# Layer 0 cross attention: key tiles taken in pairs, with another division of the PSUM banks

## What is computed

```python
def _L0_xattn_ref(x, latents, mask, g1, b1, g2, b2, Wq, Wkv, Wout):   # x: the context, latents: the normalised x
    heads, dim_head = (16, 64)
    xn, ln_lat = layer_norm(x, g1, b1), layer_norm(latents, g2, b2)
    q = ln_lat @ Wq
    kv = jnp.concatenate([xn, ln_lat], axis=1) @ Wkv
    k, v = jnp.split(kv, 2, axis=-1)
    q, k, v = (to_heads(q), to_heads(k), to_heads(v))
    scale = 1.0 / np.sqrt(np.sqrt(dim_head)).astype(np.float32)
    weight = jnp.einsum('bhld,bhnd->bhln', q * scale, k * scale)
    weight = jnp.where(full_mask[:, None, None, :], weight, neg)      # only context keys can be masked
    weight = jax.nn.softmax(weight.astype(jnp.float32), axis=-1)
    out = jnp.einsum('bhln,bhnd->bhld', weight, v)
    return out.transpose(0, 2, 1, 3).reshape(b, l, heads * dim_head) @ Wout
```

## Time and profile before

| what | value |
|---|---|
| median of 3 runs | 3242.64 us (3238.62 to 3245.68) |
| the profiled execution | 3243.5 us, its span 3241.8 us |
| mean granted TensorE clock | 0.943 |
| TensorE busy | 2901.1 us, 89% |
| VectorE busy | 1949.8 us, 60% |
| ScalarE busy | 1456.5 us, 45% |
| GpSimd busy | 1210.1 us, 37% |

### The profile page before, as it was taken

How to read it: one execution, slowest core, us unless ns; L and a number is a source line. 1 busy time by engine, 2 the same in 40 slices (tenths; PEclk the granted TensorE clock), 3 DMA queues, 4 the chain that set the end, 5 groups by cost and what they waited for, 6 DMA issues and landing times. The chain is left out here.

```text
span 3241.8 us, 48893 instructions
## 1 busy us (share of the span) xinstructions
PE 2901.1 (89%) x18490; PEld 1956.2 (60%) x18490; DVE 1949.8 (60%) x3101; ACT 1456.5 (45%) x2394; POOL 1210.1 (37%) x1001
## 2 busy tenths in 40 slices
PE   7869999999999979999998695999687888899977
PEld 6745555555555548888884564999465565344355
DVE  6556676676676754224218774555447858666576
ACT  3334444444444434324324373777333635355664
POOL 0026666666666640000004341566133403122232
PEclk9979999999999989999998896999798999799989
DMA  1100000000000002111101005666300000000010
GB/s 59 49 7 1 1 1 1 1 1 1 1 1 1 1 19 62 46 33 59 46 14 33 22 2 181 205 202 195 71 1 16 5 10 1 2 1 1 1 33 27
DMA packets 117131, 114.51 MB, mean 35 GB/s; under 512 B 22827, under 2 KB 102726, under 8 KB 116902
## 3 DMA queue, kind: packets, MB, share of 16 engines
q1 hardware_dynamic: 103173, 97.66, 9.7%
q0 software_dynamic: 7488, 9.48, 1.6%
q10 hardware_dynamic: 6240, 4.26, 0.4%
HBM read 100.81 MB, written 11.47 MB: 35 GB/s over the span
## 5 line engine op out<-in xcount | busy, mean ns | idle before, releaser
L827 POOL TENSOR_TENSOR acc<-acc,pf 128x512 f32<-128x512 f32 (+1 forms) x448 | 570.8, 1297 | 206.7 <-ACT pf L952 206.7
L1009 DVE TENSOR_REDUCE mxa<-ps 128x1 f32<-128x512 f32 x512 | 329.3, 684 | 290.3 <-PE ps L873 290.0
L952 ACT ACTIVATE pf<-ps 128x512 f32<-128x512 f32 x512 | 277.9, 595 | 278.0 <-PE ps L848 253.7
L861 PE MATMUL ps<-pf,v 128*64 128x512 f32 (+1 forms) x1152 | 311.7, 620 | 0.0
L3737 ACT ACTIVATE pT<-ps 128x1024 f32<-128x1024 f32 (+1 forms) x192 | 154.1, 811 | 134.3 <-PE ps L3654 133.8
L1204 POOL TENSOR_TENSOR x<-x,ys 128x256 f32<-128x256 f32 x16 | 11.8, 739 | 510.5 <-DVE ys L1409 510.5
L3750 DVE TENSOR_REDUCE mx<-ps 128x2 f32<-128x1024 f32 (+1 forms) x192 | 175.1, 951 | 45.4 <-PE ps L3641 37.4
L1858 POOL TENSOR_TENSOR e<-e,sm 128x1232 f32<-128x1232 f32 x48 | 107.9, 2247 | 168.3 <-DVE sm L2128 168.3
L2588 DVE TENSOR_TENSOR w_lo<-w2a,w_hi 128x2048 fp32r<-128x2048 f32 x39 | 89.4, 2292 | 101.5 <-ACT w_hi L2475 101.5
L2387 PE MATMUL ps<-xT,w1r 128*128 128x128 f32 x1248 | 148.2, 278 | 0.0
L2387 PEld LDWEIGHTS ps<-xT,w1r 128*128 128x128 f32 x1248 | 144.9, 195 | 0.0
(11 more groups left out here) (550 smaller groups left out, 7380.5 us busy)
## 6 DMA issues: line engine op xcount, KB each, us to landing
w1r<-in_f_w SPq DMA_DIRECT2D x39, 1024.0 KB, 5.1
w_raw<-in_c_h SPq DMA_DIRECT2D x32, 512.0 KB, 4.3
w2a<-in_f_w SPq DMA_DIRECT2D x8, 1024.0 KB, 13.0
w_raw<-in_c_w SPq DMA_DIRECT2D x32, 128.0 KB, 2.3
x<-in_x SPq DMA_DIRECT2D x1, 2048.0 KB, 8.2
moe_rows<-rowbuf ACTq DMA_DIRECT2D x4, 512.0 KB, 8.2
moe_acc<-x ACTq DMA_DIRECT2D x1, 2048.0 KB, 9.5
x<-moe_acc SPq DMA_DIRECT2D x4, 512.0 KB, 5.5
```

The costliest lines, as they stand in the source:

```text
L827: pool.tensor_tensor(now[0:r, :], now[0:r, :], pf[0:r, n % RING, a, :], ALU.add).then_inc(added.sem, 1)
L861: ins = pe.matmul(g.bk(3)[SIDE[a], :], v[0:r, u // 2 % 2, t, u % 2 * P + a * HD:u % 2 * P + (a + 1) * HD], pf[0:r, n % RING, a, :], start= ...
L952: act.activation(pf[0:r, n % RING, a, :], g.bk(bk.bank[f"s{n}_{a}"])[0:r, :], ACT.Exp, bias=bias)\
L1009: dve.tensor_reduce(mxa[:, q % 2, half, a, j:j + 1], g.bk(4 + a), AXX, ALU.max).then_inc(bk.release(f"m{q}_{i}_{a}"), 1)
```

## The change

The scores get four banks, two for each of two neighbouring tiles (0 to 3). The values move to bank 4, the maxima to 5 and 6, and all small products inside the loop use bank 7 alone; those ahead of the loop use banks 0 to 3 in turn. TensorE runs over pairs of tiles: scores of the next two tiles, maxima of the even one, its small product, values of both, the small product of the odd tile, its maxima. (When the even tile is the last of a chunk, its values stand ahead of the odd tile's small product and the other values behind it.) ScalarE follows the same order. VectorE takes, in an even tile, the maxima and then the small product, and in an odd tile the small product and then the maxima. The tables that place the small products, the maxima and the reciprocals change, `ahead` has five items in place of three, and a maxima item waits only for the key columns that it reads.

```diff
-        TURN_AT, SUMS_AT, SCALE_AT, Y_AT, REC_AT = 6, 1, 4, (5, 7), {2: (0, 1), 3: (2, 3)}
-        QUERY_AT, KEYS_AT = 0, {2: 0, 3: 1, 4: 2}
-        VALUES_AT = {(0, 2): 0, (0, 3): 1, (0, 4): 2, (1, 2): 3, (1, 3): 4}
+        TURN_AT, SUMS_AT, SCALE_AT, Y_AT, REC_AT = 5, 0, 4, (6, 8), {1: (0, 1), 2: (2,), 3: (3,)}
+        QUERY_AT, KEYS_AT = 2, {1: 0, 3: 1, 4: 2}
+        VALUES_AT = {(0, 1): 0, (0, 3): 1, (0, 4): 2, (1, 1): 3, (1, 3): 4}
...
-        MAXIMA_AT = {0: (1, 2), 1: (1, 3), 2: (1, 4), 3: (1, 5), 4: (1, 6), 5: (1, 7), 6: (2, 8), 7: (2, 0), 8: (2, 1)}
-        NEGATED_AT = 5
+        MAXIMA_AT = {0: (1, 4), 1: (1, 6), 2: (1, 5), 3: (1, 7), 4: (2, 0), 5: (2, 2), 6: (2, 1), 7: (2, 3), 8: (2, 8)}
+        NEGATED_AT = 3
...
-        ahead = [(1, 8), (1, 0), (1, 1)]
+        ahead = [(1, i) for i in (0, 2, 1, 3, 8)]
...
-        fills = [(misc[o], 6 + i % 2) for i, o in enumerate(others)]
-        fills += [(f"s{n}_{a}", (2 * n + a) % 3) for n in range(Q * NT9) for a in range(HN)] + [(f"o{q}", 3) for q in range(Q)]
-        fills += [(f"m{q}_{i}_{a}", 4 + a) for q, i in items for a in range(HN)]
+        fills = [(misc[o], i % 4 if i < len(opened + between) else 7) for i, o in enumerate(others)]
+        fills += [(f"s{n}_{a}", 2 * (n % 2) + a) for n in range(Q * NT9) for a in range(HN)] + [(f"o{q}", 4) for q in range(Q)]
+        fills += [(f"m{q}_{i}_{a}", 5 + a) for q, i in items for a in range(HN)]
...
-                    pe.wait_ge(*bk.read(misc["k", u, 2], 0))
+                    pe.wait_ge(*bk.read(misc["k", u, i % 2 if i < 8 else 2], 0))
...
                 scores(0)
-                for n in range(Q * NT9):
-                    q, t = divmod(n, NT9)
-                    if n + 1 < Q * NT9:
-                        scores(n + 1)
-                    for m in maxima_in(q, t):
+                scores(1)
+                for n in range(0, Q * NT9, 2):
+                    for k in (n + 2, n + 3):
+                        if k < Q * NT9:
+                            scores(k)
+                    for m in maxima_in(*divmod(n, NT9)):
                         maxima(*m)
+                    for o in others_in(*divmod(n, NT9)):
+                        other(*o)
                     values(n)
-                    for o in others_in(q, t):
+                    if n % NT9 != NK:
+                        values(n + 1)
+                    for o in others_in(*divmod(n + 1, NT9)):
                         other(*o)
+                    if n % NT9 == NK:
+                        values(n + 1)
+                    for m in maxima_in(*divmod(n + 1, NT9)):
+                        maxima(*m)
...
-                    for m in maxima_in(q, t):
-                        maxima(*m)
-                    if n:
-                        for o in others_in(*divmod(n - 1, NT9)):
-                            other(*o)
+                    if n % 2 == 0:
+                        for m in maxima_in(q, t):
+                            maxima(*m)
+                    for o in others_in(q, t):
+                        other(*o)
+                    if n % 2:
+                        for m in maxima_in(q, t):
+                            maxima(*m)
```

More of the change, by code:

```diff
@@ L860, in values @@
                         pe.wait_ge(*bk.read(f"s{n}_{a}", 0))
-                        ins = pe.matmul(g.bk(3)[SIDE[a], :], v[0:r, u // 2 % 2, t, u % 2 * P + a * HD:u % 2 * P + (a + 1) * HD], pf[0:r, n % RING, a, :],
+                        ins = pe.matmul(g.bk(4)[SIDE[a], :], v[0:r, u // 2 % 2, t, u % 2 * P + a * HD:u % 2 * P + (a + 1) * HD], pf[0:r, n % RING, a, :],
                                         start=t == 0, stop=t == NK, skip_group_check=True)
@@ L872, in maxima @@
                             j, half = divmod(i, 2)
-                            ins = pe.matmul(g.bk(4 + a), qH[SIDE[a], u % 2, cc * CH + j * P:cc * CH + (j + 1) * P],
+                            ins = pe.matmul(g.bk(5 + a), qH[SIDE[a], u % 2, cc * CH + j * P:cc * CH + (j + 1) * P],
                                             kH[SIDE[a], u % 2, half * CH:(half + 1) * CH], start=True, stop=True)
@@ L876, in maxima @@
                             for j in range(TC):
-                                ins = pe.matmul(g.bk(4 + a)[:, j * LP:(j + 1) * LP], qH[SIDE[a], u % 2, cc * CH + j * P:cc * CH + (j + 1) * P],
+                                ins = pe.matmul(g.bk(5 + a)[:, j * LP:(j + 1) * LP], qH[SIDE[a], u % 2, cc * CH + j * P:cc * CH + (j + 1) * P],
                                                 kH[SIDE[a], u % 2, S:S + LP], start=True, stop=True)
@@ L958, in heads_out @@
                         act.wait_ge(*scaled.at(0, q - 1))
-                    act.activation(oraw[:, q % 2, :], g.bk(3), ACT.Copy).then_inc(bk.release(f"o{q}"), 1)
+                    act.activation(oraw[:, q % 2, :], g.bk(4), ACT.Copy).then_inc(bk.release(f"o{q}"), 1)
                 def other(kind, x, i):
@@ L987, in _ @@
                 other("turn", 0, 0)
-                for n in range(Q * NT9):
-                    q, t = divmod(n, NT9)
-                    probabilities(n)
-                    if q and t == 0:
-                        heads_out(q - 1)
-                    if n:
-                        for o in others_in(*divmod(n - 1, NT9)):
-                            other(*o)
-                heads_out(Q - 1)
-                for o in others_in(Q - 1, NK) + tail:
+                probabilities(0)
+                probabilities(1)
+                for n in range(0, Q * NT9, 2):
+                    for k in (n + 2, n + 3):
+                        if k < Q * NT9:
+                            probabilities(k)
+                    for o in others_in(*divmod(n, NT9)):
+                        other(*o)
+                    for k in (n, n + 1):
+                        if k % NT9 == NK:
+                            heads_out(k // NT9)
+                    for o in others_in(*divmod(n + 1, NT9)):
+                        other(*o)
+                for o in tail:
                     other(*o)
@@ L1008, in maxima @@
                         if i < 8:
-                            dve.tensor_reduce(mxa[:, q % 2, half, a, j:j + 1], g.bk(4 + a), AXX, ALU.max).then_inc(bk.release(f"m{q}_{i}_{a}"), 1)
+                            dve.tensor_reduce(mxa[:, q % 2, half, a, j:j + 1], g.bk(5 + a), AXX, ALU.max).then_inc(bk.release(f"m{q}_{i}_{a}"), 1)
                     if i == 8:
                         b = q // (2 * PAIRS)
-                        cv = g.ps[:, 4:6, 0:TC * LP].rearrange("p a (j l) -> p a j l", l=LP)[:, :, :, 0:L2]
+                        cv = g.ps[:, 5:7, 0:TC * LP].rearrange("p a (j l) -> p a j l", l=LP)[:, :, :, 0:L2]
                         dve.tensor_tensor(cv, cv, mrow[:, b * L2:(b + 1) * L2].unsqueeze(1).unsqueeze(1).broadcast_to([P, HN, TC, L2]), ALU.add)\
@@ L1086, in _ @@
                             scale(q - 1)
-                for o in others_in(Q - 1, NK):
-                    other(*o)
                 for part in range(TC):
```

## The result

The changed kernel takes 3299.83 us (3297.61 to 3302.0, 4 runs) against 3243.85 (3238.62 to 3245.68, 4 runs) for the kernel before: a ratio of 1.0175 with a 95% interval from 1.0158 to 1.0193. It is slower, as forecast, but by 56 us where I had 18, and above the range. The profiled execution has a span of 3298.2 us, 56.4 more than before, and the whole of it lies in the stage that changed: the next stage's first work on ScalarE starts at 1247.5 us instead of 1190.6.

A forecast was written before the change was run, and what follows sets the result against it. TensorE was taken as the bound. Stalls and opening of 60.0 us less a 49.5 gain, plus 8.1 for longer negated maxima, gave +18.6; 3243.5 + 18.6 - 0.9 = 3261 us, range 3222 to 3284.

The forecast's parts named there:

- TensorE as the bound: In the changing stage TensorE is busy for all of 62.09 us per two chunks, so shortening its stream shortens the kernel.
- the joints: TensorE's extra time at changes of array shape; pairing tiles removes 0.35 us for each of 144 pairs, 50.4 us.
- (a): Projections in odd tiles: the maxima read behind the low half makes TensorE wait; 0.65 us each, three per head pair.
- (d): Denominators at t=0 of the odd chunk wait for the residual add of t=8: 0.56 us.
- the opening: Ahead of the loop: a wait of about 0.9 us ends, but two more maxima groups come; taken as +2.0 us.
- the sign: The whole kernel becomes slower, net +18.6 us; slower by more than 0.2% had chance 0.63.
- (b): The turn at t=5 of the even chunk waits for bank 7, held by context keys of t=4: 0.66 us.
- (c): The maxima at t=6 follow a read that stands behind the scaling of t=4: 0.17 + 0.10 us.
- t=5 of the odd chunk: Maxima there come 0.4 us late in 7 head pairs, 1.3 in the fifteenth, behind negated maxima: 4.1 us together.
- (e): At the wrap from odd to even chunk the context reads end 0.05 us late: 0.15 with the lone start.
- blocked twice: Rival: GpSimd row sums block two of the negated maxima's small instructions; 3273 us, up to 3284; chance 0.17.
- The maxima chain stays hidden: Rival: maxima reads behind low halves cost nothing, so 29.3 us go and the kernel takes 3232 us; chance 0.22.

The follow-up runs named there:

- e8: e6 with GpSimd adding only 16 of 512 columns of each row sum (leaves out most softmax denominators): 3196.39 us.
- e5: The changed kernel with the fourth reciprocal of the denominators taken at t=2 in place of t=3: 3268.05 us.
- e6: Changed kernel, maxima first except at t=8, negated maxima ahead of the odd tile's small product, context keys at t=7, fourth reciprocal at t=2: 3217.05 us.
- e1: The changed kernel with VectorE reading the maxima ahead of the small product in odd tiles too: 3297.26 us.
- e11: e9 with its early two-instruction step right behind the odd tile's maxima read, ahead of its small product: 3213.88 us.
- e10: The changed kernel with both the edit of e1 and that of e5: 3266.48 us.
- e2: The changed kernel with the 78 context columns of the keys at t=7 in place of t=4: 3303.28 us.
- e3: The changed kernel with GpSimd adding only 16 of 512 columns of each row sum (leaves out most softmax denominators): 3233.03 us.
- e7: e6 with the 78 context columns of the keys back at t=4: 3240.13 us.
- e9: e6 with the negated maxima split: two of three maxima combined and negated at t=1, one instruction left for the end: 3238.44 us.

## Why the prediction was wrong in size

Right were: TensorE as the bound; the joints, which vanish at both kinds of place; (a), 0.66 at a place against 0.65; (d), 0.56 as worked out; the opening, whose first scores come 38.8 us after its first product instead of 37.1, so +1.7 against +2.0; and the sign. In e8 the stretch is 0.29 us a pair shorter where I had 0.35, but small waits of its own are in that number; read row by row the joints are whole.

The step that failed is (b), the turn that waits for bank 7, through the length of the negated maxima. I took 1.9 us for the three small instructions and 2.4 as the longest, with at most two of them caught. Since two tiles' sums of both heads now run one after another, all three were caught: 3.1 us. The start of the turn, 0.52 behind the values in a free case, lay 2.86 behind: 2.34 us in place of 0.66 + 0.35. The bound of 2.4 rested on the reading of the earlier trace rows as a matter of instructions with two inputs, while the third of them in the earlier trace rows, at 0.17, only said that no row sum ran at that time. A row of the kernel before says so, over the stage (shortest, median, longest in ns):

```profile
L1029 DVE TENSOR_SCALAR nm<-mx x30: 174/174/1199, 245.2 to 1124.7; 128x8 f32<-128x8 f32 x30
```

Its longest, 1.2 us, is the first one, at 245.18, in a chain of 0.45, 1.19 and 1.20 us. So all three were caught once already in the kernel before, 2.8 us from start to next start, and 2.4 was no upper bound.

The second error is a term that was not in the sum. I had costed each wait at its own length, and the slow clock behind this one costs 1.5 us more each time. The rest is smaller: (c) never happened; and at t=5 of the odd chunk the maxima came 1.5 us late in all where I had 0.4, since the same negated maxima stand ahead of them:

```profile
595.87 0.99 PE L873 MATMUL ps<-kH,qH 64*128 64x512 f32 x2 [0.73 <-DVE mxa L1022]
```

1.12 us since the product before (594.75) instead of 0.23, and 0.92 to the next one (596.79) instead of 0.32.

| term | forecast, us | measured, us | difference |
|---|---|---|---|
| (b) at 15 turns | 15 x (0.66 + 0.35) = 15.2 | 14 x 2.34 + 1.5 = 34.3 | +19.1 |
| clock behind it | 0 | 11 x 1.55 = 17.0 | +17.0 |
| t=5 of the odd chunk | 4.1 + 8 x 0.35 = 6.9 | 7 x 1.5 + 2.4 = 12.9 | +6.0 |
| (c) | 15 x 0.27 = 4.0 | 0 | -4.0 |
| (e) | 15 x 0.15 = 2.3 | 15 x 0.34 = 5.1 | +2.8 |
| (a) | 45 x 0.65 = 29.3 | 45 x 0.66 = 29.7 | +0.4 |
| opening | 2.0 | 1.7 | -0.3 |

(e) is 0.10 us in the scores and 0.24 in the maxima behind them (from 606.22 and 608.17 on). The differences add up to 41.0; with the forecast of +18.6 that is 59.6, and 56.4 were measured on the spans. So the account comes out 3.2 us too high, which stays open; it is one execution of each kernel, and the opening alone takes 0.6 us more in e5 and e6, which have it unchanged.

Of the rivals, "blocked twice" was the nearest and had 0.17, up to 3284; three times blocked, without the clock, would by these rows have been about 3283 (3300 less the 17 of the clock). "The maxima chain stays hidden" was wrong as a fact, and e1 shows that it was wrong as arithmetic too: taking (a) away gave back 2.6 us and not 29, since the same VectorE chain then makes the turn wait longer and the clock falls more often. Adding up was right for the changed kernel, where each wait stands in the trace with its length; what can't be done is to take one out of the sum and keep the others. That the order rather than the pairs of tiles loses the time is shown by e6 and e11, which keep the pairs and the banks and beat the kernel before by 25 and 29 us.

## What to carry to other kernels

Before an order is changed, list the engine that works just below its limit in the new order instruction by instruction, and cost every small instruction between two of its deadlines as if each were caught once by the other engine on the shared port, not one or two of them. Where a wait of one engine hangs on a chain of another, shorten or move the chain; taking out an earlier wait of the same engine lengthens the later one and can cost the rest in clock (e1, e10), and taking out the named releaser uncovers the next (e2). And a long wait of TensorE can cost more than its length, so that a small move that keeps waits short can pay several times over (e5: 0.8 us of work moved, 31.8 us gained).

## What the runs showed of the hardware

A negation of 128x8 numbers on VectorE took 0.17 us with GpSimd free (e3, all 32) and 1.20 with row sums running. Three dependent ones in a row were each caught once, 3.1 us for 0.5 us of work, and it was enough to start 0.09 us after the row sum (e7). A maximum of two such tiles, fused with the negation into one instruction (e9), had a median of 0.18 with the row sums in place, since at most of its places none is running when it starts: being caught depends on the moment.

TensorE's granted clock fell behind waits, more often the longer they were:

| run | wait of TensorE, us | for | the clock fell |
|---|---|---|---|
| e5 | 1.47 | bank 7, turn | 0 of 14 |
| e7 | 1.57 | bank 7, context keys | 3 of 15 |
| e9 | 1.94 | bank 7, keys at t=3 | 5 of 14 |
| e10 | 2.11 | bank 7, turn | 8 of 14 |
| the changed kernel | 2.27 | bank 7, turn | 11 of 14 |
| e1 | 2.92 | bank 7, turn | 13 of 14 |

The waits of one row agree within 0.05 us, so the length of a wait does not decide alone whether the clock falls. Each fall behind a turn cost 1.5 us. Two shorter waits that follow each other can do the same: in e2 (1.01 us for the turn and, 1.4 us after its start, 0.77 for the maxima behind) the clock fell at 9 of 14. In e1 it fell also behind two of the waits of 1.2 us for the maxima of t=5 in odd chunks.
